# Loading only the non-zero corner of each Toeplitz block: four kinds of rows, five loads per ring slot instead of two

## The reference, cut to what matters

```python
# layer 1 (K = 128 taps, one filter of 128 taps for each of the 512 channels)
x_pad = jnp.pad(x, ((0, 0), (K - 1, 0), (0, 0)))
conv = conv_b + sum(x_pad[:, k:k + L, :] * conv_w[k, 0] for k in range(K))
proj = conv @ Wp + bp
B_t, C_t = softplus(proj[..., :N]), tanh(proj[..., N:])
u = x @ Ws + bs
state = decay * state + dt * B_t * u;  y = C_t * state      # scan over time
x = x + y @ Wo + bo
# layer 2
h = tanh(h @ Wh + x_t @ Wx + b)                             # 128 steps
x = x + h
```

## Time and profile before

| | |
|---|---|
| median of 3 runs | 1212.12 us (1210.01 to 1213.63) |
| the profiled execution | 1210.98 us, its span 1208.7 us |
| busy, share of the span | PE 96%, PEld 80%, DVE 58%, ACT 43%, POOL 28% |
| read from HBM, written | 103.95 MB, 33.55 MB |
| ring loads | 64 of `hankel` and 64 of `x_rev`, 512 KB each |
| ends of the stages | first matmul 6.55 us, stage 1 ends at 50.75 us, last convolution near 243 us, recurrence from about 325 us |

### The profile page before, as it was taken

The page is one execution under the profiler, slowest core; times in us unless marked ns, Lnnn a source line. Parts: engine busy times, 40 slices in busy tenths (PEclk is TensorE's granted clock), DMA queues, the critical chain, the costliest instruction groups (busy, mean ns, idle before and its releaser), DMA issues.

```text
span 1208.7 us, 15961 instructions
## 1 busy us (share of the span) xinstructions
PE 1165.7 (96%) x5984; PEld 970.3 (80%) x5984; DVE 695.8 (58%) x1078; ACT 523.5 (43%) x788; POOL 335.7 (28%) x180
## 2 busy tenths in 40 slices
PE   6899999997798999999999999999999999999997
PEld 5799999973577888888888888888888888888886
DVE  2366766669867555555555555555555555555553
ACT  2355665576533434444443343434443343444431
POOL 0000005020333333333444333333344333333340
PEclk9999999999999999999999999999999999999999
DMA  9988777711111222222222332222222332222202
GB/s 354 394 283 287 256 260 249 242 40 44 36 42 61 90 86 69 69 69 69 69 69 86 94 96 71 69 69 69 69 69 69 102 92 84 69 69 69 69 35 70
DMA packets 81422, 137.94 MB, mean 114 GB/s; under 512 B 3888, under 2 KB 39728, under 8 KB 81392
## 3 DMA queue, kind: packets, MB, share of 16 engines
q1 hardware_dynamic: 81392, 137.51, 34.8%
HBM read 103.95 MB, written 33.55 MB: 114 GB/s over the span
## 4 chain that ended last, share of the span: by engine, by line
PE 88%; DVE 7%; DMA 3%; ACT 1%; issue 0%; POOL 0%; SPq 0%; POOLq 0%; DVEq 0%
PE bank L747 10%; PE bank L755 9%; PE bank L756 9%; PE bank L759 9%; PE bank L741 9%; PE bank L740 9%; PE bank L668 9%; PE bank L795 5%; PE bank L681 4%; DMA ring<-x_rev 3%; PE bank L716 3%; PE bank L722 2%; PE bank L730 2%; PE bank L731 2%; DVE bc L545 2%; PE bank L695 2%
## 5 line engine op out<-in xcount | busy, mean ns | idle before, releaser
L355 POOL TENSOR_TENSOR x_lo<-x_f,x_hi 128x512 fp32r<-128x512 f32 x128 | 164.2, 1315 | 606.5 <-ACT x_hi L435 606.5
L464 ACT ACTIVATE h_f<-z_f 128x512 f32<-128x512 f32 x128 | 80.9, 632 | 351.7 <-DVE z_f L622 351.6
L626 DVE TENSOR_TENSOR hT_lo<-bank,hT_hi 128x512 fp32r<-128x512 f32 x128 | 88.5, 691 | 216.8 <-ACT hT_hi L468 216.7
L755 PE MATMUL bank<-wh_hi,hT_hi 128*128 128x512 f32 x512 | 200.7, 392 | 0.0
L756 PE MATMUL bank<-wh_lo,hT_hi 128*128 128x512 f32 x512 | 199.9, 390 | 0.0
L741 PE MATMUL bank<-wx_lo,x_hi 128*128 128x512 f32 x512 | 199.8, 390 | 0.0
L740 PE MATMUL bank<-wx_hi,x_hi 128*128 128x512 f32 x512 | 199.6, 390 | 0.0
L622 DVE TENSOR_TENSOR z_f<-bank,b_rows 128x512 f32<-128x512 f32 x128 | 88.5, 692 | 121.2 <-PE bank L759 120.9
L668 PE MATMUL bank<-ring 128*128 128x128 f32 x1024 | 138.7, 280 | 15.3 <-DMA ring<-x_rev 15.3
L349 POOL TENSOR_TENSOR x_lo<-x_f,x_hi 128x2048 fp32r<-128x2048 f32 x32 | 147.9, 4621 | 7.0 <-DVE soft_end L538 5.6
L747 PE MATMUL bank<-wx_hi,x_lo 128*128 128x512 f32 x512 | 145.1, 405 | 0.4 <-POOL x_lo L355 0.4
(11 more groups left out here) (83 smaller groups left out, 1578.2 us busy)
## 6 DMA issues: line engine op xcount, KB each, us to landing
ring<-hankel SPq DMA_DIRECT2D x64, 512.0 KB, 4.3
ring<-x_rev SPq DMA_DIRECT2D x64, 512.0 KB, 5.3
x_f<-x_dtb SPq DMA_DIRECT2D x32, 1024.0 KB, 8.2
out<-x_f SPq DMA_DIRECT2D x31, 1024.0 KB, 5.3
wx_f<-Wx SPq DMA_DIRECT2D x1, 1024.0 KB, 8.0
wh_f<-Wh SPq DMA_DIRECT2D x1, 1024.0 KB, 8.0
out<-x_f SPq DMA_DIRECT2D x4, 256.0 KB, 2.2
wp_f<-Wp SPq DMA_DIRECT2D x1, 384.0 KB, 9.8
```

The lines of the kernel that those rows point to most:

```text
L355: nc.gpsimd.tensor_tensor(x1_lo[:, c], x1_f[par][:, c], f(x1_hi[:, c]), ALU.subtract)\
L464: nc.scalar.activation(h_f[:], z_f[:], ACT.Tanh).then_inc(h_ready, 1)
L626: nc.vector.tensor_tensor(hT_lo[:], turned_h, f(hT_hi[:]), ALU.subtract).then_inc(htlo_ready, 1)
L755: nc.tensor.matmul(z, hT_hi[:, k], wh_hi[:, k], start=False, stop=False)
```

## The change

Row r of a Toeplitz block (r the matrix row, 0 to 127) has its first non-zero element at column 127 - r. The change sorts the rows into four kinds of 32 rows: kind k has rows 32k to 32k + 31, whose columns below 96 - 32k are zeros for all of them. Kind k is put on partitions k, k + 4, k + 8 and so on, and is loaded by a DMA of its own, from column 96 - 32k on: runs of 256, 512, 768 and 1024 bytes, 32, 64, 96 and 128 KB for kinds 0 to 3. The columns that are not loaded are set to zero once for each slot by VectorE (a memset of columns 0 to 95 on all partitions, before anything else on that engine), and SyncE waits for the slot's memset before the first load of kinds into it. x is permuted on the host to the same order of rows, so `x_rev` is loaded by one DMA as before, now ahead of the others. A ring slot counts 5 x 16.

```diff
-LOAD = 2 * 16
+KINDS = 4
+LOAD = (1 + KINDS) * 16
...
+        t_zero = sem("t_zero")
...
-        def toeplitz(n):
+        def toeplitz(row, column, n):
-            return bass.AP(hankel.tensor, n * (CH // 2 * 4 * P), [[2, P], [4 * P, CH // 2], [1, 2 * TIME]])
+            return bass.AP(hankel.tensor, 2 * (row + column) + n * (CH // 2 * 4 * P),
+                           [[2, P // KINDS], [4 * P, CH // 2], [1, 2 * (TIME - column)]])
...
-            def load_ring(n, slot):
-                sp.dma_start(ring[:, slot, 0].rearrange("p (j k) -> p j k", j=CH // 2), toeplitz(n)).then_inc(ring_loaded[slot], DMA)
+            def load_ring(n, slot, zeroed=0):
                 sp.dma_start(x_part(slot), x_rev[:, bass.ds(n * CH, CH), :]).then_inc(ring_loaded[slot], DMA)
+                wait(sp, t_zero, zeroed)
+                for kind in range(KINDS):
+                    column = P - P // KINDS * (kind + 1)
+                    sp.dma_start(t_part(slot)[kind:P:KINDS, :, column:, :].rearrange("p j l i -> p j (l i)"),
+                                 toeplitz(P // KINDS * kind, column, n)).then_inc(ring_loaded[slot], DMA)
...
             for n in range(RING):
-                load_ring(n, n)
+                load_ring(n, n, n + 1)
...
         @block.vector
         def _(dve):
+            for slot in range(RING):
+                nc.vector.memset(t_part(slot)[:, :, 0:P - P // KINDS, :], 0.0).then_inc(t_zero, 1)
...
-        "x_rev": x.transpose(1, 2, 0)[::-1],
+        "x_rev": x.transpose(1, 2, 0)[::-1].reshape(KINDS, -1, D, BATCH).swapaxes(0, 1).reshape(TIME, D, BATCH),
```

## The result

The changed kernel takes 1222.55 us (median of 4 runs, 1221.37 to 1226.64) against 1211.74 (1210.01 to 1213.63) for the kernel before, a ratio of 1.0091 (95% interval 1.0073 to 1.0109): 10.8 us slower, where 4.7 us less were forecast. The bytes did fall as the change says: HBM read is 91.36 MB in place of 103.95.

What follows compares the result with a forecast made beforehand. Load bandwidth was taken to bound stage 1; with SyncE's issues then slowest at 2.44 us a slot, it would end at 46.0 us against 50.75, and 4.7 us off the median 1212.12 gave 1207.4 us, range 1203.4 to 1215.5.

Steps and rivals of the forecast that it cites:

- What bounds the kernel: Load bandwidth paces stage 1, 2.60 us a slot; time saved there shortens the whole one for one; stage 2 is TensorE work.
- Term 2: SyncE's queue in stage 1: five issues a slot in place of two, 0.48 us each, 2.44 us with the wait.
- the 0.4 us of lag: End of stage 1: 0.4 us added because slot transfers and the load of `wp_f` would lag a little behind SyncE.
- Rival D: SyncE's issues in stage 1: 0.61 us a kind, 2.99 us a slot, 4.3 us slower, 1216.4 us; chance 0.15.
- the sign named for it: SyncE's queue in the profile after: kinds' issues of 0.56 us would point to the slower case, 0.43 to 0.45 to the forecast.
- its threshold of 0.54: SyncE's queue in stage 1: the change turns from gain to loss at 0.54 us an issue.
- Term 1: Ring loads: a slot moves 832 KB in place of 1024 and its transfers take 2.2 to 2.5 us.
- The line through the earlier trace: DMA packets of ring loads: about 6.5 ns + 0.038 ns per byte each, giving 2.2 us a slot.
- Rival C: Kinds' transfers in stage 1 are slow, 2.65 us a slot, so no change, 1212 us; chance 0.15.
- The 274 GB/s of the earlier trace: Ring loads: runs of 1 KB alone reach only 274 GB/s, cited as support for slow transfers of kinds.
- Term 3: VectorE's four memsets at the start: 0.85 us each, only the first holds anything, cost 0.4 us.
- The rule on small loads: Split ring loads: transfers under 64 KB pay mostly overhead, splitting over partition halves isn't worth it; taken to change the sum by nothing.

Runs made afterwards that it cites:

- e4: Kernel before, with four kinds on adjacent partitions only from the 17th ring load on, that is for stage 2: 1213.49 us, ratio 1.0003.
- e8: Kernel before, with hankel loaded behind x in four DMAs by pair of channels, each over all 128 partitions: 1212.94 us, ratio 1.0001.
- e9: Kernel before, with stage 2's Toeplitz blocks loaded over partitions in eight patterns in turn, all bytes: 1213.37 us against 1214.55 beside it.
- e5: Changed kernel, with kinds 0 and 1 of the first 16 slots issued from ScalarE's queue: 1209.81 us, ratio 0.9985 to the kernel before.
- e1: Changed kernel with two kinds of 64 rows, step two, in place of four: 1210.67 us, ratio 0.9980 to the kernel before.
- e6: Changed kernel with two kinds, each on 64 adjacent partitions, x in its old order: 1229.15 us, ratio 1.0120 to the kernel before.
- e2: Changed kernel with all four kinds loaded at full width from column 0, 1024 KB a slot: 1223.56 us, ratio 1.0087 to the kernel before.
- e3: Changed kernel with each kind on 32 adjacent partitions, x in its old order: 1220.60 us, ratio 1.0055 to the kernel before.
- e10: Kernel before, with rows 32 to 127 loaded full on 96 adjacent partitions, rows 0 to 31 from column 96: 1228.81 us, ratio 1.0102.

## Why the prediction was wrong, point by point

- **What bounds the kernel** held: stage 1 of the kernel before is paced by the transfers, a microsecond there is a microsecond of the whole, and stage 2 covers both more issues and fewer bytes (203.3 us in both, and e4).
- **Term 2 failed, and decided.** I priced a kind at 0.435 us, by issues directly behind a load of 128 runs, and took the number of runs as what matters. e8 shows that this price is right, five times in a row, for loads over all partitions. A kind with a step of four costs 0.60 us, and so does the x behind it: 3.22 us a slot in place of 2.40. Over 16 slots that is 13.1 us. The last issue of stage 1 began at 54.6 us and not at 40.65, and landed 2.87 us later (2.8 taken); with the 1.3 us of the lower clock and without the 0.4 us of lag that is the end at 60.9, as seen (60.98), in place of 46.0.
- **Rival D** was this case, at 0.15, and the sign named for it, kinds' issues of 0.56 us in place of 0.43 to 0.45, came, at 0.60. It took 0.61 us from one start to the next (from `wo_f` and `ws_f`), where 0.645 was seen, and x at 0.55 where it was 0.63: 2.99 us a slot in place of 3.22, 3.7 us over 16 slots. The lower clock adds 1.3 us, and the rest of the way from +4.3 to +10.2, some 0.9 us, is mostly single long issues and the one pause on SyncE's queue. No run tests its threshold of 0.54. I called `wo_f`'s 0.56 perhaps a matter of new code, because `wx_f` took 0.43. But `wo_f` goes to 64 adjacent partitions, and by e9 these cost 0.60 to 0.62, first after a wait and in a row; `wx_f`, on all 128, took 0.59 in the changed kernel, behind a kind. `wo_f` was the only row of a load that did not cover all partitions, and I wrote that no row had such a load as the change makes; with that, the nearest row was this one and not the cheapest.
- **Term 1 was too cheap as well.** The line through the earlier trace rows gave 2.2 us a slot; e5, where nothing but transfers paces, shows 2.57, while the kernel before shows 2.72 over the same slots, where the line gives 2.6. (The sum for the slot of before comes to 2.62 and not 2.64, and the line through both points has 6.9 ns, not 6.5; neither matters.) The line holds for loads over all partitions (e8: 62 ns both), and not for these: 61 ns in place of 52 for e5, 61 in place of 57 for e1 (step of two). So with issues as cheap as I took them the change would have brought some 2 us, as e5 did (a ratio of 0.9985, whose interval reaches up to 1.0000), and not 4.7.
- **Rival C** had nearly this slot (2.65) and named the crowding of engines on ports as its ground. The experiments do not show that: with a step the packets that are long are few, and they are x's too. Two of its steps were wrong. The 274 GB/s of the earlier trace rows is not what runs of 1 KB can reach, since the queue wasn't full there (its share in the same window: `q1 hardware_dynamic: 397, 0.41, 89.6%`). And with the kinds at half the full rate, 199 GB/s, they take 1.65 us and a slot 2.97, not this rival's 2.65.
- **Term 3**: the memsets took 0.70 us each (0.85 taken), the first matmul started at 6.82 us and not at 5.9: the dear issues of slot 0.
- **The rule on small loads** ("DMA: Bandwidth & Descriptors", "Rules for kernel authors", of the Trainium skill) I had set aside as changing nothing. Its bound of 64 KB is tested by no run: e8's loads, free of charge where they cover all partitions, are of 128 KB. Its other half, that a split over halves of the partitions isn't worth it, agrees with e6 (3.65 us a slot).

## What to carry to other kernels

Splitting a load by partitions can have two prices which its bytes don't show: the issuing queue's time for each part (large with a step, or with 64 adjacent partitions), and a lower rate of the transfers (much lower with adjacent partitions). Before cutting bytes that way, add up the issues of one round of the ring at the dearest row that covers fewer than all partitions, and compare with the time a round has. A split that keeps each load on all 128 partitions paid neither (e8). Two kinds (7/8 of the bytes, three issues) won 0.2% where four (13/16, five issues) lost 0.9%.

## What the runs showed of the hardware

- SyncE's time for one DMA goes by the partitions it names and by the DMA before it, not by its bytes (32 to 128 KB cost the same, e2 and the changed kernel). After a wait it is 0.31 to 0.35 us for 16, 32 or 96 adjacent partitions and for x on 128, 0.37 to 0.38 for 128 with 512 runs, and 0.60 to 0.63 for 64 adjacent and for a step of two or four. Directly behind another it is 0.43 behind 16, 32 or 128 partitions with at most 128 runs, 0.48 to 0.53 behind 96, 0.50 to 0.54 behind 128 with 512 runs, and 0.59 to 0.60 behind 64 adjacent or a step. The only load that falls out is `wo_f`, on 64 adjacent partitions with one run each: 0.51 to 0.61 in e9, e3, the kernel before and e6. 96 and 128 had the most runs, so partitions and runs aren't told apart there. Why 64 costs more than 32, 96 and 128 stays open.
- Mean time of a packet, as a ratio to the line 6.5 ns + 0.038 ns per byte, with the queue full: 128 partitions 1.00 (e8), step of two 1.06 (e1), step of four 1.16 (e5), 32 adjacent 1.47 (e3), 96 + 32 adjacent 1.46 (e10), 64 adjacent 1.59 (e6). e2, all runs 1 KB with a step of four, has 98.5% of 16 x 25 us for 5438 packets, 72 ns at 1469 bytes, 1.16 too: short runs are not the cause. With a step a few packets are long and the median stays (e5); with adjacent partitions the median itself rises (e3). Why, no trace shows.
- Two queues issue side by side at nearly their own price: 0.60 to 0.63 us an issue where one queue alone had 0.60 (e5).
